# Layer 1 of a four-layer graph network: messages scattered as three bf16 parts to sorted rows and summed by one-hot matmuls, edge counts moved to layer 3

## What is computed

```
diff = pseudo[:, None, :] - mu[None, :, :]
logw = jnp.sum(-0.5 * diff ** 2 / (1e-14 + sigma[None] ** 2), axis=-1)
gaussian = jnp.exp(logw)
msg = x[col] * gaussian
out = jax.ops.segment_sum(msg, row, num_segments=x.shape[0])
return out @ W.T + b
```

## Time and profile before

| | us |
|---|---|
| runs, lowest / median / highest of 3 | 21095.46 / 21123.57 / 21128.88 |
| the profiled execution | 21038.38 |
| its span, first to last instruction | 21036.4 |
| layer 1, first scatter-add issued to the last one's start | 650.9 to 6581.4 |
| layer 3, first to last gather's start | 12879.7 to 17807.2 |

### The profile page before, as it was taken

One profiled execution on the slowest core, in us unless ns is written; L12 is line 12 of the kernel. 1 busy time (PEld: TensorE's weight loads), 2 busy tenths in 40 slices (PEclk: granted clock), 3 DMA queues, 4 the chain that ended last, 5 costly groups with the idle time before them and its releaser, 6 DMA issues. The chain is left out here.

```text
span 21036.4 us, 290806 instructions
## 1 busy us (share of the span) xinstructions
PE 13062.5 (62%) x92471; PEld 7436.5 (35%) x92471; DVE 11190.2 (53%) x19689; ACT 3073.8 (15%) x5120; POOL 11804.8 (56%) x10055
## 2 busy tenths in 40 slices
PE   0565555555554766767776753555555555699999
PEld 0344433333333444444444431222121112355554
DVE  2565444444443777777777763332222223567777
ACT  0222222222221111111111110111111111000000
POOL 4788888888886555555555554666666665100000
PEclk6565555555556888888888876666666666899999
DMA  7344444444444222222222212333333333478887
GB/s 276 47 40 37 37 39 38 37 37 36 38 37 46 49 47 48 47 47 49 48 48 47 48 37 39 70 74 70 70 71 71 73 70 66 136 262 283 288 287 265
DMA packets 3778478, 1817.18 MB, mean 86 GB/s; under 512 B 2956641, under 2 KB 3551914, under 8 KB 3758858
## 3 DMA queue, kind: packets, MB, share of 16 engines
q1 hardware_dynamic: 1777244, 1336.91, 22.9%
q0 software_dynamic: 669312, 166.80, 10.3%
q10 hardware_dynamic: 1330864, 300.38, 7.8%
HBM read 1474.43 MB, written 392.90 MB: 89 GB/s over the span
## 5 line engine op out<-in xcount | busy, mean ns | idle before, releaser
L1992 POOL DMA_INDIRECT xg<-d_tab,s_i x3136 | 3247.5, 1036 | 2571.3 <-POOLq L1987 1477.3
L2527 POOL DMA_INDIRECT xg<-d_tab,s_i x3136 | 3021.6, 964 | 1909.6 <-issue 954.9
L2247 PE MATMUL pR<-w,H 128*128 128x384 f32 x6272 | 2706.0, 560 | 1452.1 <-PEq L2241 864.4
L1394 POOL DMA_INDIRECT d_acc<-AG,ix x1568 | 2466.6, 1573 | 527.4 <-issue 462.4
L1394 POOL DMA_INDIRECT d_acc<-T,ix x1568 | 2465.3, 1572 | 522.4 <-issue 438.7
L2915 PE MATMUL pacc<-nodes,HB 128*32 128x512 fp8e4 x47040 | 2670.3, 380 | 82.7 <-PEq L2959 82.7
L2564 DVE TENSOR_TENSOR_SCAN U<-mU,U,up 128x512 f32<-128x512 f32 x392 | 501.6, 1279 | 3358.5 <-DVEq L2563 2694.0
L2247 PEld LDWEIGHTS pR<-w,H 128*128 128x128 f32 x6272 | 1223.0, 215 | 2560.8 <-issue 2210.0
L2687 PE MATMUL hb<-U,Wbc 128*128 128x512 f32 x784 | 653.4, 929 | 2234.0 <-PEq L2681 2067.8
L1747 PE MATMUL pm<-ms,eq 128*128 128x32 f32 x6272 | 1367.1, 399 | 924.8 <-PEq L1745 922.2
L2915 PEld LDWEIGHTS pacc<-nodes,HB 128*32 128x32 f16 x47040 | 1345.0, 97 | 1281.1 <-issue 116.3
(11 more groups left out here) (338 smaller groups left out, 17493.0 us busy)
## 6 DMA issues: line engine op xcount, KB each, us to landing
packed<-d_A SPq DMA_DIRECT2D x420, 1792.0 KB
row<-d_m SPq DMA_DIRECT2D x1568, 64.0 KB
xg<-d_tab,s_i POOLq DMA_INDIRECT x6272
wrow<-d_w SPq DMA_DIRECT2D x196, 512.0 KB
d_scan<-so ACTq DMA_DIRECT2D x392, 256.0 KB
d_A<-stage ACTq DMA_DIRECT2D x97, 784.0 KB, 10.9
d_ea<-in_ea_t ACTq DMA_DIRECT2D x1, 50176.0 KB
d_exp<-T ACTq DMA_DIRECT2D x1, 50176.0 KB, 248.6
```

The costliest lines, as they stand in the source:

```text
L1394: e.indirect_dma_start(out=d_acc[i], out_offset=bass.IndirectOffsetOnAxis(ap=ix[k][:, t:t + 1], axis=0), in_=mo[k][:, t * F:(t + 1) * F], ...
L1992: e.indirect_dma_start(out=xg[k][:, t, :], out_offset=None, in_=d_tab, in_offset=bass.IndirectOffsetOnAxis(ap=s_i[n][:, t:t + 1], axis=0)) ...
L2247: last = e.matmul(pR[u % 2][:, j, 0:384], H[k][:, (2 * u + j) * P:(2 * u + j + 1) * P], w2[:, :], start=True, stop=True)
L2527: e.indirect_dma_start(out=xg[n][:, j * ST + c, :], out_offset=None, in_=d_tab, in_offset=bass.IndirectOffsetOnAxis(ap=s_i[d][:, col:col + ...
```

## The change

1. **Messages are sorted, not added, by the scatter.** A message is stored as three bf16 parts (highest, middle, lowest) and its row's low digit (`id & 127`), 49 words or 196 bytes. Its place is found from the high digit (`id >> 7`, 98 buckets) and its rank in the bucket; the ranks are kept in one PSUM tile (`rank`) that two triangular bf16 matmuls per 512 edges carry forward (`below`), ACT copies them out (`ranks_out`), and DVE picks them with a bucket one-hot of 128 x 1568 (`bucket`, `taken`, `place`). POOL issues 16 plain scatters a group with no wait between them, from four buffers `ms`, into one of four `d_msg` (quarters of 52, 48, 48 and 48 groups). `eq`, `eqb`, `sr`, `pm`, the counts of equal ids and the marks go.
2. **Units.** While quarter k is scattered, quarter k-1 is summed: one unit of 3072 rows per group in 144 of the groups. SP loads 602 KB of messages and 213 KB of flags; DVE makes 24 one-hots of the low digit (128x128), PE 24 matmuls of 96 columns, DVE 3 sums of the parts and a scan across the unit (`add_up`), ACT two copies and a store to `d_sum`. The last quarter's 42 units follow the loop (`late`), with four gathers of whole rows at its end. ACT also clears three more `d_msg` (26.5 MB each) within layer 1.
3. **Prologue.** A histogram of high digits per quarter: 16 pairs of DVE one-hots (128 x 3328 and 128 x 2048) and 1024 small matmuls, then the base places (`base`). The clears before layer 1 are `d_exp` and one `d_msg` (26.5 MB) in place of the four `d_acc` (6.4 MB).
4. **Edge counts.** All 24 chunks of `EARLY` and all of `LATE` run in layer 3, in pairs of chunks c and c+24: 20, 14, 12, 11, 10, 9 and 8 slots per step over 2, 2, 2, 2, 4, 9 and 3 chunks of 8 groups, where layer 3 had 4 (at the end 3). A group has two steps. That is 2704 slots more in layer 3; `ol` is made by one tensor_scalar per slot.

Layer 2 and layer 4 keep their work (in layer 4 two `finish` calls stand one step later).

The diff, cut to its core:

```diff
+GROUPS = (52, 48, 48, 48)
+UD = 12
+UT = 2 * UD
+NU = 44
+SPAN = 2048
+PARTS = 3
+MW = PARTS * F // 2 + 1
+BU = UD // 3
+LATE_UNITS = 42
+HB1, HB2 = 13, 8
+for _n in GROUPS:
+    assert (_n * T * P + NB * 255) // 256 <= NU * UD
...
+PAIRS = [(c0, c1, n, max(CHUNK_K[HALF + c0:HALF + c1])) for c0, c1, n in RUNS]
...
-RU = 4
+CUTS = (4, 2)
+TURNS = ((0, 0), (1, 0), (0, 1), (0, 2), (1, 1), (0, 3))
...
-    d_acc = [dram(f"d_acc{b}", (NP + P, F)) for b in range(BANKS)]
+    d_acc = [dram(f"d_acc{b}", (NP, F)) for b in range(BANKS)]
+    d_msg = [dram(f"d_msg{b}", (P * SPAN, MW)) for b in range(BANKS)]
+    d_sum = [dram(f"d_sum{b}", (1 + UD * (NU if b < BANKS - 1 else LATE_UNITS), P * F)) for b in range(BANKS)]
...
+                for i, k, s, m_ in sets():
+                    e.wait_ge(S(f"dig{i}"), 16 * ST)
+                    e.sem_inc(S(f"dig{i}"), -16 * ST)
+                    for r in range(2):
+                        if i:
+                            e.wait_ge(S(f"fnh{r}"), 1)
+                            e.sem_inc(S(f"fnh{r}"), -1)
+                        for h, (to, n) in enumerate(((tens, HB1), (units_, HB2))):
+                            last = e.tensor_tensor(to[r][0:ST * m_, :, :, :].rearrange("p x j b -> p j x b"),
+                                                   bc(bc(iotab[0:ST * m_, 0:n], 1, HX), 1, CH),
+                                                   bc(digits[i][0:ST * m_, h, :, r * HX:(r + 1) * HX], 3, n), ALU.is_equal)
+                        last.then_inc(S("nh"), 1)
+                for r in range(2):
+                    e.wait_ge(S(f"fnh{r}"), 1)
...
-                for to in d_acc:
-                    flat = to.rearrange("(p m) f -> p (m f)", p=P)
-                    e.dma_start(flat[:, 0:NB * F], blank).then_inc(S("zeros"), 16)
-                    e.dma_start(flat[:, NB * F:], blank[:, 0:F]).then_inc(S("zeros"), 16)
+                clear_messages(e, 0)
+                for k in range(BANKS):
...
-                            i = t % BANKS
-                            e.wait_ge(S(f"bank{i}"), it * 128 + (k * (T // BANKS) + t // BANKS + 1) * 16
-                                      + total.get(f"bank{i}", 0))
-                            e.sem_inc(S("past_" + e.engine.name), 1)
-                            if t == BANKS - 1:
-                                e.sem_inc(S(f"fmo{1 - k}"), 1)
-                                e.sem_inc(S(f"fix{1 - k}"), 1)
-                            e.indirect_dma_start(out=d_acc[i],
-                                                 out_offset=bass.IndirectOffsetOnAxis(ap=ix[k][:, t:t + 1], axis=0),
-                                                 in_=mo[k][:, t * F:(t + 1) * F], in_offset=None, compute_op=ALU.add
-                                                 ).then_inc(S(f"bank{i}"), 16)
...
+                            e.indirect_dma_start(out=d_msg[k],
+                                                 out_offset=bass.IndirectOffsetOnAxis(ap=ix[n][:, t:t + 1], axis=0),
+                                                 in_=ms[n][:, t % CH * ST + t // CH, :], in_offset=None
+                                                 ).then_inc(S(f"mw{n}"), 16)
...
+                    def load_unit(k, u, h):
+                        e.wait_ge(S(f"fM{h}"), 1)
+                        e.sem_inc(S(f"fM{h}"), -1)
+                        e.dma_start(M[h][:, :, :].rearrange("p u x -> p (u x)"),
+                                    d_msg[k].rearrange("(p m) x -> p (m x)", p=P)[:, bass.ds(u * (UT * MW), UT * MW)]
+                                    ).then_inc(S(f"M{h}"), 16)
...
+                        for i in range(q0_, q1_):
+                            last = e.tensor_scalar(node[h][:, i, :], keys[:, :], M[h][:, i, MW - 1:MW], None, ALU.is_equal)
...
+                        e.tensor_reduce(sums[h][:, :, 1 + c * BU:1 + (c + 1) * BU],
+                                        part[at][:, :, :].rearrange("p x (s f) -> p f x s", s=PARTS), axis=X, op=ALU.add
...
+                        e.tensor_tensor_scan(acc[h][:, :, :].rearrange("p f x -> p (f x)"), runs[h][:, :],
+                                             sums[h][:, :, :].rearrange("p f x -> p (f x)"), 0.0, ALU.mult, ALU.add).then_inc(S("av"), 1)
...
+                        e.tensor_tensor(bucket[k][:, :, :], bc(keys[:, 0:NB], 1, T), bc(hf[:, :], 2, NB), ALU.is_equal
...
+                        e.tensor_tensor(taken[:, :, :], ranked[:, :, :], bucket[k][:, :, :], ALU.mult).then_inc(S("vc"), 1)
...
+                        e.tensor_reduce(place[:, :], taken[:, :, :], axis=X, op=ALU.add).then_inc(S("vc"), 1)
...
+                    def late(h, more=True):
+                        for c in range(3):
+                            if more:
+                                nodes(1 - h, 8 * c, 8 * c + 8)
+                            join(h, c)
+                            joined(h, c)
+                        add_up(h)
+                        added(h)
...
+                    def ranks_out(c):
+                        e.wait_ge(S("rk"), 1)
+                        e.sem_inc(S("rk"), -1)
+                        e.activation(ranked[:, c * CH:(c + 1) * CH, :], rank[:, :, :], ACT.Copy).then_inc(S("re"), 1)
+                        e.wait_ge(S("re"), 1)
+                        e.sem_inc(S("re"), -1)
+                        e.sem_inc(S("rv"), 1)
...
+                    def below(k, c, begin=None):
+                        e.wait_ge(S("rv"), 1)
+                        e.sem_inc(S("rv"), -1)
+                        if begin is None:
+                            e.matmul(ranks_, later[:, :], of_bucket(k if c else 1 - k, (c - 1) % ST), start=False, stop=True,
+                                     skip_group_check=True)
+                        else:
+                            e.matmul(ranks_, final[:, :], base[:, begin, :, :].rearrange("p j b -> p (j b)"), start=True, stop=True)
+                        e.matmul(ranks_, uptob[:, :], of_bucket(k, c), start=False, stop=True, skip_group_check=True
+                                 ).then_inc(S("rk"), 1)
...
+                            last = e.matmul(part[at][:, x // 2, :], node[h][:, i, :],
+                                            M[h][:, i, 0:MW - 1].bitcast(BF16), start=(x % 2 == 0), stop=(x % 2 == 1))
...
-                        for i in range(2 if n else 0):
-                            count_ones(e, A, n, w + i)
...
+                            for which, j in TURNS:
+                                count_ones(e, A, ns, i, which, j)
...
+                            if i:
+                                for which, j in TURNS[3:]:
+                                    count_sums(e, A, ns, which, j)
                             step((i // 2 + 2) % 8, i % 2)
-                            for w in range(2 * i - 2, 2 * i + 2 if i == 15 else 2 * i):
-                                if w >= 0:
-                                    count_sums(e, A, n, w)
+                            for which, j in TURNS[:3]:
+                                count_sums(e, A, ns, which, j)
                             if i % 2:
```

969 lines of the change are left out of this document (625 added, 344 removed).

## The result

The changed kernel takes 22644.92 (22574.86 to 22650.72, 4 runs), the kernel before 21126.22 (21095.46 to 21150.09, 4 runs): a ratio of 1.072, 95% interval 1.0703 to 1.0736. It is 7.2% slower, where 3.7% faster was forecast, and outside the range. The profiled run took 22574.86, its span is 22573.1 (before 21036.4).

| stretch | before | after | difference |
|---|---|---|---|
| start to layer 1's first scatter | 650.9 | 746.8 | +96 |
| layer 1, first to last scatter | 5930.5 | 6069.7 | +139 |
| from there to layer 2's first gather (after: the 42 late units) | 84.7 | 643.9 | +559 |
| layer 2, first to last gather | 5741.7 | 5727.4 | -14 |
| from there to layer 3's first gather | 471.9 | 486.6 | +15 |

The account below looks back on a forecast made before the run. Layer 1 was taken as bound by POOL's scatters, in unit groups by DVE; layer 3 had no full engine. 21038 + 110 (prologue) - 1014 (layer 1) + 130 (layer 3) = 20264; forecast 20350, range 19,850 to 21,050.

Parts of the forecast that it names:

- A group is 16 x 1.309 = 20.9 in place of 30.27, and no scatter waits for another: Layer 1: POOL's 16 plain scatters take 20.9 per group, where scatter-adds took 30.27; 52 groups without a unit run at this.
- 144 unit groups at 23.0: Layer 1 loop: in groups with a unit, DVE's summed work and waits take 23.0, over POOL's 20.9; together 3312.
- Layer 3, +130: Layer 3: the added count slots mostly hide in the gap beside the gathers; cost +130, bounds 0 to 400.
- So the arithmetic of a group needs 12.3 ..., which leaves about 12.8: Layer 3: of 25.1 per group, set by the gather side, about 12.8 is room for the added count slots.
- Late units, 12 each: Behind layer 1's loop: 42 units with nothing beside them, 5 of exposed load and 7 of DVE each, 504 in all.
- Prologue +110: Prologue: histogram one-hots +40, key work behind the clears +47, base places +23; in all +110, bounds 0 to 170.
- The whole-row gathers, 15: End of layer 1: the whole-row gathers and the put take 15.
- Clears and loads beside the scatters at nothing: Layer 1: clears of `d_msg` and unit loads share DMA with the scatters and were costed at nothing.
- The chain in layer 1 is longer: Rival, layer 1: waits of 0.9 between ACT, PE and DVE make unit groups 26, +432, 20,780; gain gone at 28.4; chance 0.13.
- Layer 3 cannot hide the counts: Rival, layer 3: PE's queue adds each slot to the gather loop, +1300, 21,520; decides above 70% of slot time; chance 0.07.
- The port between DVE and POOL: Rival, layers 1 and 3: narrow DVE one-hots slow POOL over a shared port, unit groups 25.0, total 21,800; chance 0.03.
- The signs that were set: Prediction wrong if layer 1's DVE waits long on ACT or PE, scatters exceed 1.1, or layer 3 exceeds 26 at 9 slots.

Follow-up runs that it names:

- the isolated hand-over: Kernel without the network: two engines pass a token to and fro 256 times per stage; a PE-ACT round took 1.25 alone, 2.8 beside unspaced plain scatters.
- the thinned gathers: Changed kernel with 4 of the 16 gathers of each group of layer 3, all else kept: 21074.75.
- the gathers spaced: Kernel before with a 256-byte POOL memset before each gather of layers 2 and 3: 20051.1, ratio 0.9479.
- spacing on both sides: 256-byte POOL memset before gathers of layers 2 and 3, in the changed kernel also before layer 1's scatters: kernel before 20051.1, changed 20208.89.
- with the add: Changed kernel with scatter-adds into the cleared rows in place of layer 1's plain scatters: 22675.49.
- with the pause: Changed kernel with a 256-byte POOL memset before each scatter of layer 1 and each gather of layers 2 and 3: 20208.89, ratio 0.956.

## Why the prediction was wrong

- **The step that failed: "A group is 16 x 1.309 = 20.9 in place of 30.27, and no scatter waits for another", and with it 144 unit groups at 23.0.** The price of a scatter was right (0.972 and 0.31). With three quarters of the scatters gone the groups took the 23.0 of DVE's sum, partly by luck: DVE was busy 18.0 of it and waited 5.0, where the sum had over 21 of work and 1.7 of waits. Put together they take 33.0, and the first 52 groups 26.0 in place of 20.9, because beside plain scatters 1.28 apart the results of short matmuls are late (a round of 2.8 in place of 1.25 in the isolated hand-over), and DVE, ACT and POOL wait for PE by turns. The sum assumed that POOL's speed and the other engines' hand-overs don't touch each other. The loop was to save 1533 and takes 139 more.
- **Layer 3, +130: measured +773.** "So the arithmetic of a group needs 12.3 ..., which leaves about 12.8" took all of the gap for room. The 12.3 itself is near the 12.0 that the thinned gathers gave without slots, though those last groups of the earlier trace rows ran at a higher granted clock, 0.89 against 0.69:

```profile
17811.36:17848.22 36.86, 32.36 (x104) 12.32 (x104) 18.75 (x33) 10.38 (x19) 0.00 (x0) 0.89 0.17 34
```

The 12.0 + 0.47 per slot of the thinned run gives 30.8 with 40 slots, the forecast's 30, and 20.5 with 18, under 25.1, so the prices of the arithmetic were right. Wrong was that the rest of the 25.1 stands still when work is put into it: it held POOL's own 20.3 and some of the same delay (23.7 with the gathers spaced), and with more matmuls in each group it took 36.9 and 27.5. With spacing on both sides layer 3 costs 5022 - 4645 = +377, at the edge of the bounds of 0 to 400; the other 400 go with the delay, which is argued from this difference and not measured apart.

- **Late units, 12 each: near.** 546 for 42 is 13.0; POOL issues nothing there, and DVE waits 248 for loads, 41 before the first and 5 before each of the others, as the sum had it. **Prologue +110: near** (+96); its parts were not taken apart. **The whole-row gathers, 15: right.** **Clears and loads beside the scatters at nothing: right**, the DMA share was 0.25 and 0.32 with the groups at 23.0.
- **Rivals.** "The chain in layer 1 is longer" (0.13) names where the time shows, ACT, PE and DVE handing over, but prices each wait at its old 0.9; at 33 a group it was past its own point of 28.4. "Layer 3 cannot hide the counts" (0.07) is right in its direction and has 59% of its size (773 of 1300), under its own 70%; whether its loop over PE's queue is the way, no run shows. The port between DVE and POOL (0.03) is not what made the 33: a scatter's median is 0.972 and its mean 1.064, 1.5 a group. It was dismissed on the wrong rows, though: the one-hots that it looked at leave a scatter alone, and `bucket`, `taken` and `acc` do not, which shows where POOL sets the pace (1.675 in place of 1.555 with the add, 1.097 in place of 0.976 with the pause). No rival had an engine that is slowed in its hand-overs by a third one.
- **The signs that were set** did their work: "DVE in layer 1 shows long waits on ACT or PE" came, and layer 3 ran at 27.5, over 26, with 9 slots a step. The third, scatters over 1.1, did not come.
- **In the earlier trace rows the sign had been there before.** POOL waited 184 times for a buffer in layer 3 although DVE was busy 150 of 500 and PE 272 of 500: a stage in which nobody is full, beside plain gathers 1.27 apart. Layer 1 showed none of it, with its scatter-adds 1.89 apart. The change took that away.

What stays open is the resource inside the chip. Shown is that the spacing decides, not bytes or DMA share; that the steps are of 0.70, in the isolated hand-over; and that the delay builds up and drains: it came 34 us after the first close scatter and went 26 us after the last. A queue that fills when DMAs follow each other too closely and holds up the engines' messages would fit, but it does not hold the DMAs' data, which had all moved by then, and no run looks into it. One rival is untested: each execution here has a recorded span of its own, so the recording was on in all of them, and with 2.8 for a round with one weight load and one matmul and 22.4 for a round with eight of each the delay goes by the instruction, as it would if the recording were what is late. No run has the recording off, so it is not shown that the delay, or the gain from the pause, is there without it.

## What to carry to other kernels

Look at the spacing of POOL's plain indirect DMAs: where it is under some 1.4 us for long and other engines hand work to each other in small pieces, idle time on all engines at once and a consumer that starts many us after the matmul that it waits for (16 here) are the sign, and a pause on POOL is worth trying. The length of the wait instructions is no sign: in the loop of the changed kernel ACT's wait for `rank` is 0.017 all 784 times. Here a memset of 0.33 before each gather, work that nobody needs, made the kernel before 5.2% faster, and the change, even spaced, stayed 0.8% behind it. And before an engine's own price is taken as a loop's bound, ask whether it was measured beside the same neighbours.
